# The FFN's up products by Strassen's seven block products, its down sums kept in SBUF, its narrow tile first

## The reference

```python
mod = (silu(c) @ wmod).reshape(2, 6, 1, -1)
sa, ca, ga, sb, cb, gb = (mod[:, i] for i in range(6))
ga, gb = (sign(g) * max(abs(g), 0.25) for g in (ga, gb))
h = layernorm(x) * (1 + ca) + sa
x = x + ga * (h @ masked(weight).T + bias)
h = layernorm(x) * (1 + cb) + sb
# lora_linear(x, w, a, b) = x @ w.T + 2 * (x @ a.T) @ b.T
g = silu(lora_linear(h, w1, A1, B1)) * lora_linear(h, w3, A3, B3)     # hidden size 1376
x = x + gb * lora_linear(g, w2, A2, B2)
```

## Time and profile before

| | us |
|---|---|
| median of 3 runs (264.52 to 265.27) | 264.66 |
| the profiled execution | 267.26 |
| its span, first to last instruction | 265.7 |
| TensorE busy | 248.6 |
| VectorE busy | 125.5 |
| ScalarE busy | 86.5 |
| GpSimd busy | 61.7 |

### The profile page before, as it was taken

How to read it: one execution, slowest core, us unless ns; L and a number is a source line. 1 busy time by engine, 2 the same in 40 slices (tenths; PEclk the granted TensorE clock), 3 DMA queues, 4 the chain that set the end, 5 groups by cost and what they waited for, 6 DMA issues and landing times.

```text
span 265.7 us, 3341 instructions
## 1 busy us (share of the span) xinstructions
PE 248.6 (94%) x1205; PEld 197.6 (74%) x1205; DVE 125.5 (47%) x208; ACT 86.5 (33%) x144; POOL 61.7 (23%) x75
## 2 busy tenths in 40 slices
PE   7799975989989999999999999999999999999990
PEld 6577773668768888888888877888888888888770
DVE  3516864669979985475465542351222112220144
ACT  2326776063624346545633320111111011110100
POOL 1326789512632313123201000060000000000012
PEclk9979998999999999999999999999999999999997
DMA  6999930006122341322324600037000000000004
GB/s 186 388 381 417 407 129 1 5 2 215 58 100 79 121 118 41 121 79 63 95 81 122 34 3 2 0 16 156 28 0 0 1 2 0 0 0 2 0 0 158
DMA packets 12371, 23.99 MB, mean 90 GB/s; under 512 B 1218, under 2 KB 2498, under 8 KB 12356
## 3 DMA queue, kind: packets, MB, share of 16 engines
q1 hardware_dynamic: 12208, 23.65, 28.9%
q10 hardware_dynamic: 148, 0.14, 0.2%
HBM read 21.16 MB, written 2.10 MB: 88 GB/s over the span
## 4 chain that ended last, share of the span: by engine, by line
PE 79%; DVE 6%; ACT 5%; issue 4%; DMA 2%; POOL 2%; SPq 0%; DVEq 0%; ACTq 0%; POOLq 0%
PE up_a L1050 21%; PE up_b L1050 21%; PE acc L1064 8%; PE acc L1065 8%; PE acc L1063 8%; PE acc L1001 4%; DMA xt<-in_x 2%; PE side L1031 2%; ACT ht_hi L513 1%; DVE stats L652 1%; PE acc L907 1%; ACT work L496 1%; PE side L919 1%; PE side L1035 1%; DVE parts L732 1%
## 5 line engine op out<-in xcount | busy, mean ns | idle before, releaser
L846 DVE TENSOR_TENSOR g<-up_b,g 128x512 f32<-128x512 f32 (+1 forms) x22 | 15.2, 690 | 73.2 <-PE up_b L1050 73.2
L1064 PE MATMUL acc<-w_lo,g_hi 128*128 128x512 f32 (+1 forms) x88 | 34.7, 394 | 0.0
L1065 PE MATMUL acc<-w_hi,g_lo 128*128 128x512 f32 (+1 forms) x88 | 34.7, 394 | 0.0
L1063 PE MATMUL acc<-w_hi,g_hi 128*128 128x512 f32 (+1 forms) x88 | 34.6, 394 | 0.0
L408 POOL TENSOR_TENSOR xt<-work,xt 128x512 f32<-128x512 f32 x5 | 6.8, 1382 | 112.7 <-DVE work L771 112.7
L756 DVE SCALAR_TENSOR_TENSOR raw<-side,raw 128x512 f32<-128x512 f32 (+2 forms) x33 | 21.4, 676 | 24.0 <-PE side L1031 17.4
L622 ACT ACTIVATE g<-up_a 128x512 f32<-128x512 f32 (+1 forms) x22 | 13.1, 597 | 59.5 <-PE up_a L1050 59.5
L627 ACT ACTIVATE g_hi<-g 128x512 fp32r<-128x512 f32 (+1 forms) x22 | 13.9, 632 | 52.9 <-DVE g L846 52.9
L544 ACT ACTIVATE w_hi<-raw 128x512 fp32r<-128x512 f32 (+2 forms) x33 | 20.1, 625 | 22.9 <-DVE raw L756 22.9
L1050 PE MATMUL up_a<-ht_hi,w_hi 128*128 128x512 f32 (+1 forms) x88 | 24.4, 398 | 0.4 <-ACT w_hi L544 0.4
L1050 PE MATMUL up_a<-ht_hi,w_lo 128*128 128x512 f32 (+1 forms) x88 | 24.1, 395 | 0.0
(11 more groups left out here) (151 smaller groups left out, 352.1 us busy)
## 6 DMA issues: line engine op xcount, KB each, us to landing
raw<-in_ffn SPq DMA_DIRECT2D x33, 256.0 KB, 2.6
wmod_sb<-in_wmod SPq DMA_DIRECT2D x4, 1024.0 KB, 11.1
xt<-in_x SPq DMA_DIRECT2D x8, 256.0 KB, 8.4
wmod_sb<-in_wmod SPq DMA_DIRECT2D x1, 2048.0 KB, 15.4
out<-xt SPq DMA_DIRECT2D x8, 256.0 KB, 2.9
mask_sb<-in_mask SPq DMA_DIRECT2D x4, 256.0 KB, 10.5
wa<-in_weight SPq DMA_DIRECT2D x4, 256.0 KB, 10.6
lora_raw<-in_lora SPq DMA_DIRECT2D x2, 320.0 KB, 8.2
```

Source lines behind the costliest of these rows:

```text
L846: nc.vector.tensor_tensor(g[0:w], up_b[0:w], g[0:w], ALU.mult).then_inc(g_ready, 1)
L1063: nc.tensor.matmul(acc[t][:], hi, down_hi[j][0:w], start=(j == 0), stop=False)
L1064: nc.tensor.matmul(acc[t][:], hi, down_lo[j][0:w], start=False, stop=False)
L1065: last = nc.tensor.matmul(acc[t][:], lo, down_hi[j][0:w], start=False, stop=(j == HT - 1))
```

## The change

The narrow hidden tile of 96 comes first, and the other ten are taken in PAIRS = 5 pairs. For a pair and for each of the two up matrices (a unit u = 2 i + m, ten in all) the two batches are the two block rows of the input, the two halves of the features its block columns, and the two hidden tiles the block columns of the weights. The four block results come from seven block products instead of eight: `p1` .. `p7`, each of 2 feature blocks x 3 = 6 matmuls of 128x512. VectorE adds the products to partial sums in SBUF (`add_u2`, `add_u3`, `add_c22`, `add_c21`, `add_c12`), and ScalarE copies the first (`p1_copy`). Sums of the inputs (`token_sums`, `token_sum_3`, `token_sum_4`, with their own high and low parts of 1024 columns) are made once, on VectorE and GpSimd; sums of the weights (`weight_sums`, `weight_sums_after`) for each pair on GpSimd. Seven weight blocks a pair have high and low parts, in ten slots used in turn.

Since all tokens of both batches meet a pair at once, the down product has eight token tiles a pair, and only three PSUM banks: each pair's sum is added to an SBUF buffer by VectorE (`down_add`). For the last pair `down_end` multiplies by the gate and adds what `out_prepare` on GpSimd made of the earlier sums and x. Batch 1's second layer norm is no longer spread over the FFN's steps; it is turned whole after the first product. The low part of the gated activations and three of its four products move to GpSimd (`g_low`, `g_mult`). The DMA ring for raw weights has 8 slots instead of 4. The matrices' hidden rows are reordered on the host so that the narrow tile leads.

The core of the diff:

```diff
@@ TensorE @@
+            def product(u, v, dst, hi, lo, hi_ready, lo_ready, start, signal):
+                i, m = divmod(u, 2)
+                at = block_slot(i, v)
+                if hi_ready and u == 0:
+                    pe.wait_ge(*hi_ready)
+                pe.wait_ge(w_high_ready, item_of(i, v) + 1)
+                for n, (w_part, h) in enumerate([(block_hi, hi), (block_lo, hi), (block_hi, lo)]):
+                    if n == 1:
+                        pe.wait_ge(w_ready, item_of(i, v) + 1)
+                    if n == 2 and lo_ready and u == 0:
+                        pe.wait_ge(*lo_ready)
+                    for k in range(KT // 2):
+                        last = nc.tensor.matmul(dst[:], w_part[at][:, k, m], h[:, k], start=(start and n == 0 and k == 0),
+                                                stop=(n == 2 and k == KT // 2 - 1), skip_group_check=True)
+                last.then_inc(signal, 1)
+            def p2_product(u):
+                pe.wait_ge(p1_ready, u + 1)
+                product(u, B21, up_a, ht_hi[0][:, 2:4], ht_lo[0][:, 2:4], None, None, False, p2_out)
...
+            def down(i, place):
+                n = LAST_ORDER[place] if i == PAIRS - 1 else place
+                g = group_of(i, place)
...
+                    pe.wait_ge(g_low_ready, 4 * i + (3 if b else 4))
...
+            merge(2)
+            merge(3)
             attend_last(1)
...
+            up0(0, 0, up_a, h1_out)
+            merge(4)
+            up0(0, 1, up_b, h3_out)
+            p1_product(0)
+            merge(5)
+            p2_product(0)
+            turn(12)
+            turn(13)
+            turn(14)
+            turn(15)
+            p1_product(1)
+            merge(6)
+            p2_product(1)
+            for n in range(T):
+                down(-1, n)
+            merge(7)
+            merge(8)
+            pe.wait_ge(g11_ready, 1)
+            up0(1, 0, up_a, h1_out)
+            up0(1, 1, acc[0], h3_out)
+            for i in range(PAIRS):
+                u = 2 * i
...
+                if i:
+                    p1_product(u)
+                p6_product(u)
+                if more:
+                    merge(r)
+                if i:
+                    p2_product(u)
...
+                u = 2 * i + 1
+                if i:
+                    p1_product(u)
+                p6_product(u)
+                if i:
+                    p2_product(u)
+                p5_product(u)
+                p7_product(u)
+                if i:
+                    down(i - 1, 4)
+                    down(i - 1, 5)
+                p4_product(u)
+                p3_product(u)
+                if i:
+                    down(i - 1, 6)
+                    down(i - 1, 7)
+            for place in range(TILES):
+                down(PAIRS - 1, place)
@@ ScalarE @@
+            def g_high(i, n):
+                b, e = ((0, 0), (1, 1), (1, 0), (0, 1))[n]
+                if n == 0:
+                    act.wait_ge(g11_ready, i + 1)
+                else:
+                    act.wait_ge(g_by_pool, 3 * i + n)
+                if i:
+                    act.wait_ge(down_out, group_of(i - 1, TILES if b else T))
...
+                nc.scalar.activation(g_hi[b][e][:], cbuf[:, n], ACT.Copy).then_inc(g_high_ready, 1)
...
+            silu0(0)
+            weight_high(item_of(0, B21))
+            norm(3 * T)
+            norm(3 * T + 1)
+            p1_copy(0)
...
+            p1_copy(1)
+            weight_high(item_of(0, T1))
+            weight_high(item_of(0, T2))
+            for n in range(T):
+                down0_copy(n)
+            silu0(1)
+            weight_high(item_of(0, T3))
+            weight_high(item_of(0, T4))
+            weight_high(item_of(0, B22))
+            token_high(S2)
...
+            for i in range(PAIRS):
+                if i:
+                    p1_copy(2 * i)
...
+                g_high(i, 0)
+                if more:
+                    weight_high(item_of(i + 1, T3))
+                g_high(i, 1)
+                if more:
+                    weight_high(item_of(i + 1, T4))
+                g_high(i, 2)
+                if more:
+                    weight_high(item_of(i + 1, B22))
+                g_high(i, 3)
@@ VectorE, from low(11) on @@
+            merge(2)
+            merge(3)
+            attn_gate(4)
+            attn_gate(5)
+            weight_low(2)
+            weight_low(item_of(0, B11))
+            attn_gate(6)
+            attn_gate(7)
+            add_x1(6)
+            add_x1(7)
+            moment(12)
+            moment(13)
+            merge(4)
+            moment(14)
+            moment(15)
+            weight_low(item_of(0, B21))
+            centres(12)
+            g0(0)
+            norm(14)
+            norm(15)
...
+            low(14)
+            low(15)
+            g11(0)
+            merge(5)
+            merge(6)
+            token_sums()
+            lora_part(3)
+            lora_part(4)
+            merge(7)
+            merge(8)
+            weight_low(item_of(0, T1))
+            weight_low(item_of(0, T2))
+            token_sum_4()
+            weight_low(item_of(0, T3))
+            weight_low(item_of(0, T4))
+            weight_low(item_of(0, B22))
+            token_low(S2)
+            token_low(S1)
+            add_u2(0)
+            g0(1)
...
+                add_c21(u)
+                if more:
+                    weight_low(item_of(i + 1, T4))
+                add_c12(u)
+                if more:
+                    weight_low(item_of(i + 1, B22))
+                if i:
+                    down_add(i - 1, 6)
+                    down_add(i - 1, 7)
@@ GpSimd @@
+            def out_prepare(n):
+                b, t = divmod(n, T)
+                pool.wait_ge(down_added, group_of(PAIRS - 2, n) - TILES + 1)
+                pool.wait_ge(gate_row_loaded[b], 16 * KT)
+                nc.gpsimd.tensor_tensor(out_sum(n), out_sum(n), gate_row[:, b], ALU.mult).then_inc(out_scaled, 1)
+                pool.wait_ge(out_scaled, n + 1)
+                nc.gpsimd.tensor_tensor(out_sum(n), out_sum(n), xt[:, b, t], ALU.add).then_inc(out_ready, 1)
...
+            low(12)
+            low(13)
+            g0_low(0)
+            weight_sums(0)
+            token_sum_3()
+            weight_sums_after(0)
+            spread(3)
+            spread(4)
+            token_low(S3)
+            token_low(S4)
+            g0_low(1)
+            for i in range(PAIRS):
+                if i + 1 < PAIRS:
+                    weight_sums(i + 1)
+                    weight_sums_after(i + 1)
+                else:
+                    for n in range(T):
+                        out_prepare(n)
+                if i + 2 < PAIRS:
+                    spread(2 * i + 5)
+                    spread(2 * i + 6)
+                g_low(i, 0)
+                g_mult(i, 0)
+                g_low(i, 1)
+                g_mult(i, 1)
+                g_low(i, 2)
+                g_mult(i, 2)
+                g_low(i, 3)
+            for n in range(T, TILES):
+                out_prepare(n)
+            for n in LAST_ORDER:
                 if n in X2_POOL:
                     add_x2(n)
```

More of the change, by code:

```diff
@@ L59, with stream, stream_of, item_of @@
 PASSES = [(0, 0), (1, 0), (0, 1), (1, 1)]
[L62 to L74, removed]
-FILL_TURN, FILL_COLS, FILL_H = 3, 3, 2
[L79 to L90, removed]
+CHUNKS = NORMS
+LOW_DVE = (8, 9, 10, 11, 14, 15)
+WHOLE_DVE = (9, 11, 12, 13, 14, 15)
+X1_POOL = (0, 1, 2, 4, 5)
+LAST_ORDER = (4, 5, 6, 7, 0, 1, 2, 3)
+X2_POOL = (4, 5, 6, 0, 1)
+B11, B21, T1, T2, T3, T4, B22 = range(BLOCKS)
+ITEMS = BLOCKS + 2
+S2, S1, S3, S4 = range(4)
+FILL_TURN, FILL_COLS, FILL_H = 3, 3, 2
+def stream(r):
+    if r < 3:
+        return 0, r
+    i, m = divmod(r - 3, 6)
+    return (2 * i + 1 + m // 2, m % 2) if m < 4 else (2 * i + m - 3, 2)
+def stream_of(i, m):
+    return 3 + 6 * i + m
+def item_of(i, v):
+    return 3 + ITEMS * i + v
+def group_of(i, n):
+    return TILES * (i + 1) + n
 def build(nc, x, mask, weight, bias, ffn, lora, wmod, consts, out):
@@ L278, in merge_bank, with whole_place @@
         def merge_bank(r):
-            return side[r] if r < FIRST_MERGES else side[SIDE[("merge", r)] % 2]
+            return side[r % 2]
+        def whole_place(q):
+            i, k = divmod(q, KT)
+            return hbuf[:, q % 2] if i < 2 else (h0, h1)[i - 2][:, k]
         def low_done(q):
@@ new lines, in token_sum_4, with token_low, add_u2 @@
+            def token_sum_4():
+                dve.wait_ge(s2_ready, KT // 2)
+                for c in range(KT // 2):
+                    nc.vector.tensor_tensor(h0[:, 2 + c], h0[:, 2 + c], s2_sum[:, c], ALU.subtract).then_inc(s4_ready, 1)
+            def token_low(v):
+                src = {S2: s2_sum[:], S1: h1[:, 2:4]}[v]
+                dve.wait_ge(s_high_ready, v + 1)
+                nc.vector.tensor_tensor(s_lo[v][:], src, f32(s_hi[v][:]), ALU.subtract).then_inc(s_low_by_dve, 1)
+            def add_u2(u):
```

(14 more changed lines are left out.)

720 lines of the change are left out of this document (484 added, 236 removed).

## The result

The changed kernel takes 318.27 us (317.48 to 320.97) where the kernel before takes 264.75: a ratio of 1.204, 95% interval 1.196 to 1.211. It is slower by a fifth, as forecast: 322 was predicted, with a range of 300 to 338. The profiled execution took 317.48 us, its span is 315.6.

The account below looks back on a forecast made before the run. TensorE's queue was taken as the bound. TensorE's end: 259.1 - 14.0 + 25.8 + 5.0 + 3 x 6.2 + 5.4 + 10.2 = 310.1; the chained replay's 288 + 35 gave span 323, forecast 322 us, range 300 to 338.

Parts of the forecast that it names:

- the loop: Before p2 of pairs 2, 3, 4: TensorE stands still 6.2 us each, waiting for p1_copy behind ScalarE's g_high chain.
- the stall ahead of the last block: Before the final downs: TensorE waits 5.4 us for g_low(4,2) after the old pair's downs end.
- the way in: From attention's last block into the first pair: TensorE waits sum to 25.8 us, 10.3 of them in p6_product(0).
- Removed work: Up products of ten full hidden tiles: 420 matmuls instead of 480, 14.0 us off, all on the path.
- Pair 1: Before p2 of pair 1: no older down group, yet p1_copy(2) comes 5.0 us late (3 to 8).
- The clock: After six long waits TensorE's clock falls, 1.7 us lost each: 10.2 us (0 to 15).
- The way out: From the last product's end to the span's end: 35.0 us, with about 16 us of GpSimd beyond the final downs.
- my signs of being wrong: Pairs at 32 to 34 us, VectorE SBUF instructions at 0.69 us beside GpSimd, or TensorE's last matmul within 7 us of end.
- the chained replay: Queues replayed in sequence: p2(2) at 142.5, then 39.6 us a pair, last product's end at 287.8, taken as 288.
- Faster, since the queue stays full: Rival, chance 0.06: TensorE's queue stays full, span 265; faster needs less than 14 us of waits in all.
- A clock that stays up: Rival sharing chance 0.17 with the milder port: no loss from the clock, 312; both together 295.
- A milder port: Rival sharing chance 0.17 with the clock: VectorE and GpSimd don't lock each other out, 305; both together 295.

Follow-up runs that it names:

- the kernel with the four moves: Changed kernel with old downs early, p1_copy ahead of g_high(i,3), p1_copy(0) ahead of the norms, out_prepare of tiles 4 to 7 on VectorE: 278.7 us, ratio 1.052.
- The first experiment: Changed kernel with all four old down groups ahead of p4 and p3 in TensorE's queue in a pair's second half: 303.3 us.

## Why the prediction was right, and where its sizes were off

It held in direction, in size, in the loop and in the stall ahead of the last block. It failed in the way in and in the path of the end, and the closeness of the size owes something to luck. Point by point:

- **Removed work.** 60 matmuls, as counted. Their 14 us show only in the kernel with the four moves.
- **The loop.** 6.2 us of idle ahead of p2 in pairs 2 to 4 were predicted, 5.66, 5.66 and 5.88 measured, released by the chain named; from the first g_high to p2 the trace has 8.6 us. The first experiment moved the anchor and nothing else, and the wait shrank with it.
- **Pair 1.** 5.0 predicted, 5.07 measured.
- **The way in.** 25.8 us predicted; the waits shown above and the small ones between 110 and 125 us add up to about 16. p2_product(0) has 4.93 (5.3 predicted), p5 1.21 (1.4), down(-1,0) 1.64 (1.4). The term that was mis-sized is p6_product(0): 10.3 predicted, 0.48 + 2.34 measured. I had put all 27.6 us of SBUF instructions into one queue ahead of token_low(S2). It ended at 103.7 and not at 110.8; VectorE's row:

```profile
102.49 1.21 DVE L1072 TENSOR_TENSOR s_lo<-s_sum,s_hi 128x1024 fp32r<-128x1024 f32 x1
```

  Of these 7.1 us, 2.8 are a slower start of the profiled execution of before (its turns began at 56.97, here at 54.14). For the other 4.3 two terms of the queue stand out: GpSimd's first 1024-wide low part (2.6) began only at 104.06, behind it, and of the four spreads (2.4) the three that began ahead of it cost VectorE 0.3 us. p2_product(2) came at 134.3 where the replay had 142.5, so 5.4 us earlier beyond the start.
- **The clock.** 1.7 us a long wait predicted from one idle stretch of 3.1 us; 2.2 measured in the loop. Stalls that I charged nothing for had it too: ahead of the last block (granted clock 0.72 from 290 to 296 us) and of its last group (0.50 from 306 to 310). TensorE's busy time, 252.4 us, is 17.8 more than 248.6 less the removed 14.0; I had charged 10.2. With about 40 instead of 39.6 us a pair it took back a little of the error above.
- **The way out.** 5.4 us of wait ahead of the last block, 5.39 measured; 35.0 us from the last product's end to the span's end, about 33.7 measured (281.9 to 315.6). The path of it was wrong in part. I had TensorE done some 16 us before GpSimd; but VectorE's queue holds the last groups' banks until GpSimd's out_prepare are through, which costs TensorE the 4.60 us, a wait that the sum doesn't have. TensorE's last matmul ends 6.4 us before the span, which was one of my signs of being wrong (within 7 us), and VectorE, not GpSimd, ends last.
- **Luck in the sum.** TensorE's end was added up to 310.1, and it came at 309.2. The way in was 10 us shorter and everything began 2.8 us earlier; the wait of 4.60 and about 8 us more of low clock filled that up. The forecast itself went by the chained replay: 8.2 us too late at p2_product(2), some 2.3 too short from there to the last product, 1.3 too long at the end, 7.2 of the span in all. The forecast is only 3.7 above the measured median, as I had taken 2.6 off for it.
- **The rivals.** "Faster, since the queue stays full" failed by its point of decision, less than 14 us of waits: there were 16 in the way in alone. A clock that stays up is out. A milder port is out for the 128x512 instructions (weight_low at 1.34 to 1.37 us) and holds for the small spreads (0.3 us for three); the rest of what was milder is the order in which the engines get the port.

What stays open: of the 13 us that the kernel with the four moves is behind, how much is VectorE's and GpSimd's work between 80 and 110 us and how much the end. A version that beats the kernel before wasn't found.

## What to carry to other kernels

Removing work from the busiest engine pays only while that engine stays fed: here 14 us of matmuls were saved and some 60 us of waits and low clock taken in (46 us more idle, 17.8 of low clock), though no other engine was busy more than 60% of the span. Before such a change, follow every buffer that is used again round the loop: what must be read before it is overwritten, on which queue the reader stands, and what stands behind the writer; a copy queued behind an unrelated chain cost 5.7 us a pair, and moving it together with the old downs cost nothing. At the end, look for an engine whose in-order queue waits for the slow one while it holds banks that a third needs. Work moved to an engine that shares a port with a busy neighbour should be priced with the neighbour's queue, and its order against it treated as unknown.

## What was not expected of the hardware

- A run of VectorE's two-input SBUF instructions can hold GpSimd off for long: one instruction of 0.6 us took 6.87 where six instructions were moved off GpSimd. Elsewhere GpSimd's small ones got in between, at 1.3 to 1.85 us each, and cost VectorE a tenth of a microsecond.
- The same idle doesn't always have the same price. 3.1 us of idle (attention in the kernel before) and 3.03 in the first experiment brought the clock down, 3.02 and 3.25 in the same execution of that experiment didn't; after 5.66 us it was at half for 6 us once and for 2.9 the next time.
